# A fused attention and FFN kernel: the two loads of wk issued from ScalarE's queue instead of SyncE's

## The chip, the cores and the metric

The kernel runs on one core of a Trainium2 chip. The metric is the device time of one execution in microseconds (us), as a median over runs.

## The reference

Cut to what matters here: a cross attention with 8 heads of 128 and a context of 2 x 77 rows, then a feed-forward layer (a shared expert and a gate that is almost always shut).

```python
def _L0_xattn_ref(x, context, Wq, Wk, Wv, Wo, bo):
    q = (x @ Wq).reshape(B, Tq, h, C) * SCALE          # x is layer-normalised, 2 x 1024 x 256
    k = (context @ Wk).reshape(B, Tk, h, C) * SCALE    # context is 2 x 77 x 192
    v = (context @ Wv).reshape(B, Tk, h, C)
    attn = jax.nn.softmax(jnp.einsum('bqhc,bkhc->bhqk', q, k), axis=-1)
    out = jnp.einsum('bhqk,bkhc->bqhc', attn, v).reshape(B, Tq, h * C)
    return out @ Wo + bo
x = x + _L0_xattn_ref(_layernorm(x, axis=-1), ctx_768, ...)
x = x + _L0_ffn_ref(_layernorm(x, axis=-1), ...)
```

Wk and Wv are 192 x 1024 in float32 and Wq is 256 x 1024.

## The kernel before

Each engine runs a program of its own, written out by hand in the order in which it executes, and the engines meet at semaphores. The names: SyncE (SP) issues every load and store; TensorE (PE) multiplies; VectorE (DVE), ScalarE (ACT) and GpSimd (POOL) do the elementwise work.

The kernel has a stage of preparation (about the first 30 us of the profile) and then a loop over 16 tiles of 128 rows of x. The change lies at the very start of the preparation:

- TensorE multiplies a constant with itself 9 times (line 501), which needs no load, and then forms k for all 8 heads in `context_rows` (lines 350 and 356): for i = 0 it waits for the first load of wk, forms heads 0 to 3, waits for the second load of wk, and forms heads 4 to 7. The same is done with wv. Each of these four groups is 8 matmuls in the program. "K0", "K1", "V0" and "V1" stand for them below.
- ScalarE copies k and v out of the accumulators (lines 644 and 648). Its first instruction on the engine is the load of an activation table.
- VectorE takes the mean out of wq, in two halves (lines 929, 931 and 933), each half as soon as its load (`wqt_sb`, 512 KB) is in.
- TensorE then forms `a` = wq times k in `make_a` (line 369): heads 0 to 3 wait for the first half of wq, heads 4 to 7 for the second (`wq_ready`). ScalarE and VectorE split each `a` into two parts (lines 652 and 938), and the scores of the first tiles follow (lines 375 to 377).

The loads of this stage are issued by SyncE in the order ctx, wk (2 x 384 KB), wv (2 x 384 KB), wq (2 x 512 KB), then the first columns and rows of x, wo and the rest. Each load has a semaphore of its own, so a load that comes in earlier or later than its neighbour changes only when its own reader starts.

Of the kernel before, what the change touches and what calls it, by code (L numbers as in the profile page):

```python
# [43 lines left out]
def program(nc, x, x_t, ctx_p, wq_t, wk_p, wv_p, wo, bo, ws1, ws2, w1, w2, wr, out):  # L44
# [3 lines left out]
    HG = H // 2  # L48
    WB = wk_p.shape[2] // P
    E, _, FE = w1.shape  # L50
    DCH = D // P
    BK = B * TK
# [19 lines left out]
    with ExitStack() as ctx:  # L72
        def sb(name, shape, dt=F32):
            return ctx.enter_context(nc.sbuf_tensor(name, shape, dt))
# [4 lines left out]
        def sem(name):  # L79
            return ctx.enter_context(nc.semaphore(name))  # L80
# [34 lines left out]
        wk_sb = sb("wk_sb", [P, 2, WB, P])  # L115
# [59 lines left out]
        wk_in = [sem(f"wk_in{i}") for i in range(2)]  # L175
# [105 lines left out]
        @block.sync  # L281
        def _(sp):
            sp.dma_start(ctx_sb[:, :, :], ctx_p).then_inc(ctx_in, 16)
            for i in range(2):
                sp.dma_start(wk_sb[:, i, :, :].rearrange("p e c -> p (e c)"), wk_p[:, i, :]).then_inc(wk_in[i], 16)
            for i in range(2):
                sp.dma_start(wv_sb[:, i, :, :].rearrange("p e c -> p (e c)"), wv_p[:, i, :]).then_inc(wv_in[i], 16)
            for i in range(2):
                sp.dma_start(wqt_sb[:, i * H // 2:(i + 1) * H // 2, :],
                             wq_t.rearrange("(h p) d -> p h d", p=P)[:, i * H // 2:(i + 1) * H // 2, :]).then_inc(wq_in[i], 16)  # L290

            def load_x_t(i):
                for c in range(DCH):
                    sp.dma_start(xt_sb[:, c, :, i * GB * P:(i + 1) * GB * P],
                                 xt_rows[:, c, :, i * GB * P:(i + 1) * GB * P]).then_inc(xt_in[i], 16)

            def load_x(i):
                for b in range(B):
                    sp.dma_start(x_pairs[:, i * GB:(i + 1) * GB, b, :], x_rows[:, i * GB:(i + 1) * GB, b, :]).then_inc(x_in[i], 16)

            load_x_t(0)
            load_x(0)
            sp.dma_start(wo_sb[:, :, :], wo.rearrange("(h p) d -> p h d", p=P)).then_inc(wo_in, 16)
            sp.dma_start(wsr_sb[:, :, 0:FE], ws1.rearrange("(c p) f -> p c f", p=P)).then_inc(wsr_in, 16)
            sp.dma_start(wsr_sb[:, :, FE:NL], wr.rearrange("(c p) e -> p c e", p=P)).then_inc(wsr_in, 16)
            sp.dma_start(bo_sb[:, :], bo.rearrange("(a d) -> a d", a=1).broadcast_to([P, D])).then_inc(bo_in, 16)
            sp.dma_start(ws2_sb[:, :], ws2).then_inc(ws2_in, 16)
            for i in range(1, 4):
                load_x_t(i)
                load_x(i)  # L310

            def keep_x1(k):

                sp.wait_ge(x1_ready, 2 * k + 2)
                sp.dma_start(x1_sb[:, bass.ds(2 * k, 2), :], x1_tr[:, :, :]).then_inc(x1_kept, 16)

            def store(k):
                sp.wait_ge(y_ready, 2 * k + 2)
                sp.dma_start(out_rows[:, k, :, :], y_sb[:, bass.ds(2 * k, 2), :]).then_inc(y_out, 16)

            keep_x1(0)
            with sp.Fori(1, NB) as k:
                keep_x1(k)
                store(k - 1)
            for b in range(B):
                sp.wait_ge(y_ready, 2 * (NB - 1) + b + 1)
                sp.dma_start(out_rows[:, NB - 1, b, :], y_sb[:, 2 * (NB - 1) + b, :]).then_inc(y_out, 16)
            sp.wait_ge(y_out, 16 * (NB + 1))

            sp.wait_ge(gs, GATE_STEPS)  # L330
            any_open = sp.value_load(flag[0:1, 0:1], min_val=0, max_val=1)
            with sp.If(any_open > 0):
                sp.dma_start(w1_sb[:, :, :, :].rearrange("p e c f -> p (e c) f"),
                             w1.rearrange("e (c p) f -> p (e c) f", p=P)).then_inc(w12_in, 16)
                sp.dma_start(w2_sb[:, :, :], w2.rearrange("e p d -> p e d")).then_inc(w12_in, 16)
                with sp.Fori(0, NB) as k:
                    sp.wait_ge(r_acc, 2 * k + 2)
                    sp.dma_start(out_rows[:, k, :, :], y_sb[:, bass.ds(2 * k, 2), :]).then_inc(r_out, 16)
                sp.wait_ge(r_out, 16 * NB)
# [254 lines left out]
        def _(act):  # L594
# [43 lines left out]
            def hi_of_u(b, i):  # L638
                act.wait_ge(u_ready[b], i + 1)
                act.activation(u_hi[:, b, 2 * i:2 * i + 2, :].rearrange("p c d -> p (c d)"), u_bank[b, i][:, :], ACT.Copy).then_inc(uhi_ready[b], 1)  # L640

            for g in range(H // 2):
                act.wait_ge(kt_ready, g + 1)
                act.activation(kt_sb[:, 2 * g:2 * g + 2, :].rearrange("p h n -> p (h n)"), s_ps[:, g, 0:2 * BK],
                               ACT.Copy, scale=SCALE2).then_inc(kt_copied, 1)
# [445 lines left out]
```

## Time and profile before

| | us |
|---|---|
| median of 3 runs | 119.76 |
| lowest and highest of the runs | 119.48, 120.51 |
| the profiled execution | 119.6 |
| its span, first to last instruction | 117.8 |

The span is what the trace shows; 1.8 us of the profiled execution lie around it. In the trace TensorE is busy 110.2 us of the span, VectorE 89.2, ScalarE 85.0 and GpSimd 62.4. Starts in all rows count from the beginning of the span. A row of the trace that has a releaser ("[0.54 <-DVE wqt_sb L933]") tells how long the engine had been idle and which event ended that. A multiplication of float32 shows as two rows of TensorE.

### The profile page before, as it was taken

The page shows a single profiled execution, that of the slowest core. Times are in us where ns is not written, and L with a number is a line of the kernel's source. Part 1 is how long each engine was busy: PE and PEld are TensorE (multiplying, and loading weights), DVE is VectorE, ACT ScalarE, POOL GpSimd, SP SyncE. Part 2 cuts the span into 40 slices and gives each one's busy share as a digit, 9 for nine tenths or more (in the row PEclk, how much of TensorE's full clock was granted, in tenths as well). Part 3 has the DMA queues.
Part 4 walks back from the last instruction along what each step waited for, and adds up shares of the span by engine and source line. Part 5 has one row for each costly group of instructions (what it writes and reads, how often), then busy time and mean ns, then how long its engine had stood idle before and what let it go on. Part 6 is the DMA issues. An engine that isn't in the chain of part 4 may idle for free.

```text
span 117.8 us, 3097 instructions
## 1 busy us (share of the span) xinstructions
PE 110.2 (94%) x848; PEld 105.3 (89%) x848; DVE 89.2 (76%) x341; ACT 85.0 (72%) x346; POOL 62.4 (53%) x101
## 2 busy tenths in 40 slices
PE   6999989999899989999999999999999999989950
PEld 6988879998798889999999999999999999978940
DVE  0005999997799697887979797797979778687692
ACT  4025554699559879898998899898978989895200
POOL 2000451479607865786666577757647863429320
PEclk9999999999999999999999999999999999999998
DMA  3999999990000110022004001300400030040033
GB/s 104 341 323 362 347 327 349 351 331 34 0 6 3 49 40 0 6 103 75 0 0 178 0 0 70 108 0 0 178 0 0 37 141 3 3 178 0 26 125 116
DMA packets 11351, 12.70 MB, mean 108 GB/s; under 512 B 976, under 2 KB 9808, under 8 KB 11344
## 3 DMA queue, kind: packets, MB, share of 16 engines
q1 hardware_dynamic: 11344, 12.62, 32.4%
q8 instruction: 3, 0.05, 0.2%
q14 instruction: 4, 0.03, 0.1%
HBM read 8.42 MB, written 2.10 MB: 89 GB/s over the span
## 4 chain that ended last, share of the span: by engine, by line
PE 63%; DVE 20%; DMA 8%; issue 3%; ACT 2%; SPq 2%; DVEq 0%; ACTq 0%
PE o_ps L375 7%; PE o_ps L377 7%; PE o_ps L376 7%; PE s_ps L375 6%; PE s_ps L377 6%; PE s_ps L376 6%; DMA wqt_sb<-in_wq_t 6%; PE g_ps L431 6%; PE f_ps L461 5%; DVE ut_sb L953 3%; DVE row_max L804 2%; PE g_ps L444 2%; DVE wqt_sb L933 2%; PE f_ps L375 2%; DVE wq_mean L929 2%
## 5 line engine op out<-in xcount | busy, mean ns | idle before, releaser
L619 ACT ACTIVATE probs<-s_ps,neg_max,rstd 128x77 f32<-128x77 f32 x128 | 51.5, 425 | 8.2 <-DVE neg_max L812 8.2
L722 POOL TENSOR_TENSOR probs<-probs,recip 128x308 f32<-128x308 f32 x32 | 22.4, 701 | 24.5 <-DVE recip L818 24.3
L619 ACT ACTIVATION_READ_ACCUMULATOR probs<-s_ps,neg_max,rstd 128x1 f32 x128 | 27.3, 214 | 0.0
L375 PE MATMUL o_ps<-u_hi,pt_hi 128*128 128x256 f32 (+1 forms) x80 | 22.7, 284 | 1.1 <-DVE pt_lo L830 0.6
L377 PE MATMUL o_ps<-u_lo,pt_hi 128*128 128x256 f32 (+1 forms) x80 | 22.3, 279 | 0.0
L376 PE MATMUL o_ps<-u_hi,pt_lo 128*128 128x256 f32 (+1 forms) x80 | 22.3, 279 | 0.0
L375 PE MATMUL s_ps<-a_hi,xt_hi 128*128 128x308 f32 x64 | 22.0, 344 | 0.0
L377 PE MATMUL s_ps<-a_lo,xt_hi 128*128 128x308 f32 x64 | 19.5, 304 | 0.0
L376 PE MATMUL s_ps<-a_hi,xt_lo 128*128 128x308 f32 x64 | 19.4, 303 | 0.0
L375 PEld LDWEIGHTS o_ps<-u_hi,pt_hi 128*128 128x128 f32 (+1 forms) x80 | 15.0, 188 | 1.7 <-issue 0.8
L376 PEld LDWEIGHTS o_ps<-u_hi,pt_lo 128*128 128x128 f32 (+1 forms) x80 | 15.1, 188 | 0.0
L377 PEld LDWEIGHTS o_ps<-u_lo,pt_hi 128*128 128x128 f32 (+1 forms) x80 | 15.0, 188 | 0.0
L845 DVE TENSOR_TENSOR x_tr<-o_ps,xb_sb 128x256 f32<-128x256 f32 x16 | 6.8, 424 | 10.3 <-PE o_ps L377 10.3
L704 POOL TENSOR_TENSOR xt_lo<-xt_sb,xt_hi 128x256 fp32r<-128x256 f32 x16 | 12.5, 781 | 2.2 <-POOL xt_hi L702 0.2
L804 DVE TENSOR_REDUCE row_max<-s_ps 128x8 f32<-128x616 f32 x16 | 12.4, 775 | 0.2
L376 PEld LDWEIGHTS s_ps<-a_hi,xt_lo 128*128 128x128 f32 x64 | 12.1, 190 | 0.0
L375 PEld LDWEIGHTS s_ps<-a_hi,xt_hi 128*128 128x128 f32 x64 | 12.1, 189 | 0.0
L377 PEld LDWEIGHTS s_ps<-a_lo,xt_hi 128*128 128x128 f32 x64 | 12.0, 188 | 0.0
L726 POOL TENSOR_TENSOR xb_sb<-x_sb,bo_sb 128x256 f32<-128x256 f32 x16 | 11.7, 736 | 0.0
L431 PE MATMUL g_ps<-ident,probs 128*128 128x128 f32 x76 | 11.5, 273 | 0.2 <-POOL probs L722 0.2
L830 DVE TENSOR_TENSOR pt_lo<-g_ps,pt_hi 128x512 fp32r<-128x512 f32 x14 | 9.6, 687 | 1.6 <-ACT pt_hi L604 1.1
L604 ACT ACTIVATE pt_hi<-g_ps 128x512 fp32r<-128x512 f32 x14 | 8.4, 600 | 1.2 <-PE g_ps L431 1.2
(148 smaller groups left out, 249.1 us busy)
## 6 DMA issues: line engine op xcount, KB each, us to landing
xt_sb<-in_x_t SPq DMA_DIRECT2D x8, 256.0 KB, 6.7
x_sb<-in_x SPq DMA_DIRECT2D x8, 256.0 KB, 7.0
x_sb<-x_tr SPq DMA_DIRECT2D x8, 256.0 KB, 2.4
out<-y_sb SPq DMA_DIRECT2D x7, 256.0 KB, 2.3
wqt_sb<-in_wq_t SPq DMA_DIRECT2D x2, 512.0 KB, 7.5
wo_sb<-in_wo SPq DMA_DIRECT2D x1, 1024.0 KB, 9.4
wk_sb<-in_wk_p SPq DMA_DIRECT2D x2, 384.0 KB, 4.3
wv_sb<-in_wv_p SPq DMA_DIRECT2D x2, 384.0 KB, 5.6
```

Of the source, the lines that this page charges most:

```text
L375: pe.matmul(out_ap, hi, rhs_hi, start=first, stop=False)
L376: pe.matmul(out_ap, lo, rhs_hi, start=False, stop=False)
L377: return pe.matmul(out_ap, hi, rhs_lo, start=False, stop=last)
L431: mm = pe.transpose(to, probs[:, par, c * P:(c + 1) * P], ident[:, :])
L604: act.activation(pt_hi[:, 0:PB], g_ps[:, 0:PB], ACT.Copy).then_inc(pthi_ready, 1)
L619: e = act.activation(probs[:, par, h * TK:(h + 1) * TK], s_ps[:, 2 * par + half, (h - half * H // 2) * TK:(h - half * H // 2 + 1) * TK], A ...
L704: pool.tensor_tensor(xt_lo[:, par, :, :], src, xt_hi[:, par, :, :].bitcast(F32), ALU.subtract).then_inc(xt_ready, 1)
L722: pool.tensor_tensor(rows, rows, recip[:, par, hs].unsqueeze(2).broadcast_to([P, H // 2, TK]), ALU.mult).then_inc(probs_ready, 1)
L726: pool.tensor_tensor(xb_sb[:, par, :], x_sb[:, t, :], bo_sb[:, :], ALU.add).then_inc(xb_ready, 1)
L804: dve.tensor_reduce(row_max[:, par, :].rearrange("p (i h) -> p i h", i=2), s_ps[:, 2 * par:2 * par + 2, 0:HALF].rearrange("p i (h k) -> p ...
L830: dve.tensor_tensor(pt_lo[:, 0:PB], g_ps[:, 0:PB], pt_hi[:, 0:PB].bitcast(F32), ALU.subtract).then_inc(ptlo_ready, 1)
L845: dve.tensor_tensor(x1_tr[:, par, :], o_ps[:, 0:D], xb_sb[:, par, :], ALU.add).then_inc(x1_ready, 1)
```

## The change

The two loads of wk leave SyncE's program, where they stood between ctx and wv, and are issued by ScalarE as the first thing in its program. Their source, destination and semaphores stay the same.

```diff
         def _(sp):
             sp.dma_start(ctx_sb[:, :, :], ctx_p).then_inc(ctx_in, 16)
-            for i in range(2):
-                sp.dma_start(wk_sb[:, i, :, :].rearrange("p e c -> p (e c)"), wk_p[:, i, :]).then_inc(wk_in[i], 16)
             for i in range(2):
                 sp.dma_start(wv_sb[:, i, :, :].rearrange("p e c -> p (e c)"), wv_p[:, i, :]).then_inc(wv_in[i], 16)
...
+            for i in range(2):
+                act.dma_start(wk_sb[:, i, :, :].rearrange("p e c -> p (e c)"), wk_p[:, i, :]).then_inc(wk_in[i], 16)
             for g in range(H // 2):
                 act.wait_ge(kt_ready, g + 1)
```

At the start of ScalarE's list of instructions the difference is this (lines of the kernel's source shift by two or three between the versions; "x2" is a count):

```order
-L593 UNCONDITIONAL_BRANCH
+L591 UNCONDITIONAL_BRANCH
+L641 DMA wk_sb<-in_wk_p 128x768 x2
 L644 ACT_TABLE_LOAD
 L644 ACTIVATE kt_sb<-s_ps 128x308 x4
```

The two issues stand ahead of the load of the activation table, which was ScalarE's first instruction. SyncE's list begins like this before the change:

```order
L281 UNCONDITIONAL_BRANCH
L283 DMA ctx_sb<-in_ctx_p 128x308
L285 DMA wk_sb<-in_wk_p 128x768 x2
L287 DMA wv_sb<-in_wv_p 128x768 x2
L289 DMA wqt_sb<-in_wq_t 128x4x256 x2
L294 DMA xt_sb<-in_x_t 128x2x256 x2
```

and like this with the change:

```order
L281 UNCONDITIONAL_BRANCH
L283 DMA ctx_sb<-in_ctx_p 128x308
L285 DMA wv_sb<-in_wv_p 128x768 x2
L287 DMA wqt_sb<-in_wq_t 128x4x256 x2
L292 DMA xt_sb<-in_x_t 128x2x256 x2
```

All that stood behind wk on SyncE's queue stands two issues further ahead. The instructions of TensorE, VectorE and GpSimd are the same in both versions.

## Rows read from the trace of the kernel before

**Rows 1.** The page: busy time of each engine, and the chain that ended last.

```profile
PE 110.2 (94%) x848; PEld 105.3 (89%) x848; DVE 89.2 (76%) x341; ACT 85.0 (72%) x346; POOL 62.4 (53%) x101
...
PE 63%; DVE 20%; DMA 8%; issue 3%; ACT 2%; SPq 2%; DVEq 0%; ACTq 0%
```

**Rows 2.** The chain that ended last, 0 to 19 us: start, length, what.

```profile
3.06 6.98 DMA wqt_sb<-in_wq_t
...
10.07 1.23 DVE wq_mean L929
...
14.38 1.37 DVE wqt_sb L933
...
15.79 1.32 PE g_ps L369 x8
```

**Rows 3.** TensorE's instructions in order of time: start, length, line, operation, count.

```profile
1.06 3.88 PE L501 MATMUL f_ps<-mean_of 128*128 128x128 f32 x18 [1.06 <-DVE probs L924]
5.05 1.28 PE L350 MATMUL s_ps<-ctx_sb,wk_sb 128*128 128x154 f32 x8
...
6.99 1.31 PE L350 MATMUL s_ps<-ctx_sb,wk_sb 128*128 128x154 f32 x8
...
8.95 1.31 PE L350 MATMUL g_ps<-ctx_sb,wv_sb 128*128 128x154 f32 x8
...
10.92 0.79 PE L350 MATMUL o_ps<-ctx_sb,wv_sb 128*128 128x154 f32 x4
...
12.89 2.36 PE L369 MATMUL s_ps<-kt_sb,wqt_sb 128*128 128x154 f32 x16
15.79 1.32 PE L369 MATMUL g_ps<-kt_sb,wqt_sb 128*128 128x154 f32 x8 [0.54 <-DVE wqt_sb L933]
```

**Rows 4.** SyncE's DMA issues in order of time: start, time to issue, line.

```profile
0.74 0.39 SPq L283 DMA_DIRECT2D ctx_sb<-in_ctx_p  x1
1.19 0.89 SPq L285 DMA_DIRECT2D wk_sb<-in_wk_p  x2
2.12 0.91 SPq L287 DMA_DIRECT2D wv_sb<-in_wv_p  x2
3.06 1.51 SPq L289 DMA_DIRECT2D wqt_sb<-in_wq_t  x2
```

**Rows 5.** Loads of wk (line 285): time from issue to landing.

```profile
DMA to landing us min/median/max: 3.7/4.3/4.8
```

**Rows 6.** Loads of wv (line 287): time from issue to landing.

```profile
DMA to landing us min/median/max: 5.3/5.6/6.0
```

**Rows 7.** Loads of wq (line 289): time from issue to landing.

```profile
DMA to landing us min/median/max: 7.0/7.5/8.0
```

**Rows 8.** Stretches: engines' busy time, then granted clock, DMA engines' busy share, GB/s.

```profile
1.50:1.75 0.25, 0.25 (x3) 0.25 (x3) 0.00 (x0) 0.25 (x1) 0.07 (x1) 1.00 0.06 15
1.75:2.00 0.25, 0.25 (x3) 0.25 (x3) 0.00 (x0) 0.25 (x1) 0.00 (x0) 1.00 0.86 158
2.00:3.00 1.00, 1.00 (x7) 1.00 (x6) 0.00 (x0) 0.02 (x1) 0.00 (x0) 1.00 1.02 277
3.00:4.00 1.00, 1.00 (x7) 1.00 (x6) 0.00 (x0) 0.00 (x0) 0.00 (x0) 1.00 0.91 289
4.00:7.00 3.00, 2.90 (x23) 2.42 (x22) 0.00 (x0) 0.00 (x0) 0.00 (x0) 1.00 1.00 334
...
10.04:26.00 15.96, 15.42 (x117) 14.41 (x116) 15.21 (x34) 9.79 (x36) 6.63 (x10) 1.00 1.11 345
```

**Rows 9.** ScalarE's instructions in order of time, 0 to 15 us.

```profile
0.74 1.28 ACT L644 ACT_TABLE_LOAD   x1 [0.74 <-PEq L1085]
7.08 0.75 ACT L644 ACTIVATE kt_sb<-s_ps 128x308 f32<-128x308 f32 x2 [5.06 <-PE s_ps L356]
```

**Rows 10.** Waits of engines for loads, 10 to 30 us: total, times, longest.

```profile
POOL xt_hi L699 <- DMA xt_sb<-in_x_t: 11.5, 1, 11.5
...
ACT ws_hi L656 <- DMA ws_sb<-in_ws: 0.3, 1, 0.3
```

## The prediction

> **What bounds the kernel now.** I read the page first. TensorE is busy for 94% of the span and holds 63% of the chain that ended last; loads hold 8% of it [rows 1]. The change touches loads, so the question is where that 8% lies. The chain in order of time answers: nearly all of it is one piece, 6.98 us from 3.06 to 10.04, the first load of wq [rows 2]. Behind it comes VectorE's work on both halves of wq, without a gap from 10.07 to 15.75, and then TensorE's second half of `make_a` at 15.79. After that the chain goes through engines only. The waits for loads after 10.07 us are GpSimd's for x, which ended when its work began at 13.11 against scores that start at 17.89, and one of 0.3 us of ScalarE [rows 10]; neither is on the chain. So the change can act in the first 16 us alone, and what decides is the moment when TensorE starts the second half of `make_a`: 15.79.
>
> Two strands lead to that moment. The one on the chain is wq: landing, VectorE, 15.79. The other is TensorE itself: the warm-up of line 501 ends at 1.06 + 3.88 = 4.94, K0 starts at 5.05, K1 at 6.99, V0 at 8.95, V1 at 10.92, the first half of `make_a` at 12.89 [rows 3]. The groups follow each other every 1.96 us with no room between them. The first half of `make_a` lasts 2.36 us, to 15.25, and then TensorE waits 0.54 us for VectorE (the bracket of the last row of [rows 3]). That 0.54 us is the slack of TensorE's strand, and it is also the most that an earlier wq can give.
>
> Next, when the loads land. SyncE issues ctx at 0.74, wk at 1.19 and about 1.64, wv at 2.12 and about 2.59, wq at 3.06 [rows 4] (the second of a pair half of its 0.9 us later). With the times to landing [rows 5 to 7]: wk at 1.19 + 3.7 = 4.89 and 1.64 + 4.8 = 6.44, wv at 2.12 + 5.3 = 7.42 and 2.59 + 6.0 = 8.59, wq's first half at 3.06 + 7.0 = 10.06 (10.04 in the chain). K0 starts 0.16 us behind its load, which is also just behind the warm-up; K1 starts 0.55 us behind its load, V0 1.53 and V1 2.33.
>
> **The change part by part.**
>
> SyncE loses two issues, 0.89 us [rows 4], and wv, wq and all behind them are issued some 0.93 us sooner. wq is the load on the chain, so at first sight 0.54 us are to be had. But the loads don't wait for their issue. The DMA engines are idle until 1.75 us, 0.86 busy in the next quarter of a us, and about fully busy from 2 us until 26 [rows 8]. wq's first half is behind 154 + 4 x 384 KB of other loads, and these are the same bytes with the change, all wanted from the same engines. What can come sooner is only what the DMA engines would otherwise not have done before 1.9 us, and ctx, which starts the stream, is still issued at 0.74. I take 0 for wq's gain, with 0.54 us as its other end.
>
> The Trainium skill says the same against this change (DMA: Bandwidth & Descriptors, section "Issuing engines are not separate DMA queues"): DMAs of several issuing engines run on the same DMA engines and interleave, and only issue time of the sequencer is saved. By that rule wq gains nothing; by the count of issues alone it would gain all that TensorE's strand allows. The trace agrees so far as it goes: the DMA engines, not the issues, are full from 1.75 us on [rows 8].
>
> ScalarE gains two issues ahead of its table load. Taken at SyncE's price, 0.89 us, its table load moves from 0.74 to about 1.65 and ends at about 2.95. The copy of k that needs it starts at 7.08 [rows 9], so the cover is 4.1 us, and the cost is nothing. Without that cover it would be the 0.9 us.
>
> What moves on the path is the order in which wk and wv land. Before, wk had the DMA engines for itself, with wv behind it on the same queue. Now wk and the stream ctx, wv, wq lie on two queues and are served at the same time. No row of the trace has two queues with loads, so I bound it. The four loads of wk and wv are alike, 384 KB each, and in whatever order they are served the places at which one of them is complete stay about 4.89, 6.44, 7.42 and 8.59. The second wk can keep the second place (6.44) or fall to the last (8.59). I take the third, 7.42: ScalarE's and SyncE's first instructions start at the same 0.74 [rows 4, 9], so the first wk meets only ctx, as before, and keeps 4.89; then the second wk and the first wv share the DMA engines and both are in when the third place is reached.
>
> The sum for that: K0 starts at 5.05 as before, its weights being multiplied right behind the warm-up. K1 needs 7.42, plus the step of some 0.14 us from landing to matmul that K0 shows (4.89 to 5.05, of which the warm-up may hold a part): 7.56 in place of 6.99, 0.57 us late. V0 and V1 follow at their 1.96 us; their loads (7.42 at the latest and 8.59) are in well before 9.5 and 11.5. The first half of `make_a` ends at 15.25 + 0.57 = 15.82 in place of 15.25, and the second half starts there in place of 15.79: 0.03 us. The slack of 0.54 us takes up the rest. On the profiled execution that is 119.6 + 0.03; it stands 0.16 us under the median of the runs, which I carry along: 119.76 + 0.03, so **119.8 us**. The bounds from the same rows are -0.54 us (the second wk keeps its place and wq gains all) and, with the second wk last and the first second, the first rival's +1.2.
>
> **The rivals.**
>
> *The first wk has to share too* (slower). If ScalarE's first load gets going only when ctx is through, it shares with the first wv from its beginning, the two are complete at the second place, 6.44, and the second wk and wv at 8.59. K1 then waits until 8.59 + 0.14 = 8.73, 1.74 us late, and with 0.54 us of slack the second half of `make_a` is 1.2 us late: 121.0. If ScalarE's queue is served after all of SyncE's wv, the first wk comes at 7.42: K0 2.5 us late, less 0.54: 2.0 us, 121.7. This mechanism costs something from a second wk that lands after 7.4 or a first wk after 5.4, and over 1% from 8.6 and 6.6. For it: the DMA engines are full, and whoever shares them loses. Against it: the same start of both sequencers. The Trainium skill (the same page, section "Queues, rings and completion order") says that each DMA engine takes a packet in turn from each queue that has work. Worked out from that as an estimate, one packet of wk for one of ctx and then one for one of wv gives the third place, so 0.03 us, and the first wk is held up only if it starts late; no run here shows it yet.
>
> *wq comes sooner* (faster). If two queues fill the DMA engines better than one (from 2 to 4 us they move 277 and 289 GB/s, and 334 from 4 to 7 [rows 8], so one queue may leave something open) and wk is not pushed back, VectorE starts up to 0.54 us sooner with effect: 119.2. Against it: TensorE's strand must then not slip at all, though wk now shares.
>
> *The change doesn't do what it says.* If the table load ran first, wk would be issued at 2.02 and the first wk would land at 2.02 + 3.7 = 5.72 at best. K0 is then 0.8 us late, 0.3 us more than the slack: 120.1. The list of instructions speaks against it, the issues stand first.
>
> **How the numbers follow.** Third place, no change: 0.6, at 119.8, with 119.4 to 120.2 as its own range from the spread of the runs. The first wk shares: 0.2, at 121.0 or a little under, and wk behind all of wv 0.05, at 121.7. wq sooner: 0.1, at 119.2. Table load first: 0.05, at 120.1. A measurement of this kernel can tell about 1% (1.2 us) from no change. The faster end lies at -0.54 us, under half of that, so faster by over 1% gets 0.02, for what I have not seen. Slower by over 1% needs the second branch of the first rival, or its first with the noise against it: 0.1. Within 1%: 0.88. The range goes from the fast rival, 119.2, to the first one's price, 121.0.
>
> **What the profile of the changed kernel would show.** If I am right: K0 starts at about 5.05, the second K group about half a us late behind its load, wk's second load lands at 7.3 to 7.5 and wv's first beside it; wq's first half still lands at about 10.0 although its issue stands at about 2.1, so its time to landing grows by the 0.9 us that its issue gained; and TensorE's wait of 0.54 us ahead of the second half of `make_a` is gone, while that half starts within 0.2 us of 15.79. From there to the end all is as before. A K1 that starts after 8.5, or a K0 after 5.5, would show the first rival; a wq half that lands before 9.6 the second. The prediction would also be wrong if TensorE's clock fell in the new gap: it stays granted at 1.00 through the last gap of 0.54 us [rows 3, 8], but a gap of 1 us or more right behind the warm-up is in no row. At the lower of its two levels K1, V0 and V1 would take longer by their own 1.96 us each at most.

## The result, and the profile after

The changed kernel takes 119.36 us in the median (119.01 to 119.94, 20 runs) against 120.05 for the kernel before (119.32 to 120.51, 20 runs): a ratio of 0.9951, 95% interval 0.9934 to 0.9967. It is about 0.6 us faster, half a per cent. Within 1%, as forecast, but the forecast was no change, and the gain is clear of the measurement. The profiled execution took 119.25 us, against 119.6.

The page of the changed kernel: span, busy time, and the chain that ended last.

```profile
span 117.5 us, 3097 instructions
...
PE 109.9 (94%) x848; PEld 105.1 (89%) x848; DVE 89.3 (76%) x341; ACT 85.3 (73%) x346; POOL 62.4 (53%) x101
...
PE 70%; DVE 15%; DMA 7%; issue 2%; ACT 2%; ACTq 0%; DVEq 0%; SPq 0%
```

The load of wq has left the chain, which held 8% of loads in [rows 1]. In its place stands another load. The chain of the changed kernel, in order of time (start, length, what):

```profile
1.18 6.11 DMA wk_sb<-in_wk_p
...
7.33 1.31 PE s_ps L348 x8
...
13.30 2.29 PE s_ps L367 x16
15.60 1.05 PE g_ps L367 x8
```

The second load of wk ends at 1.18 + 6.11 = 7.29, and from there the chain goes through TensorE alone, K1, V0, V1 and both halves of `make_a`, without a piece of VectorE. TensorE's instructions in order of time (lines 350 and 369 of before are 348 and 367 here):

```profile
1.06 3.73 PE L499 MATMUL f_ps<-mean_of 128*128 128x128 f32 x18 [1.06 <-DVE probs L924]
5.22 1.29 PE L348 MATMUL s_ps<-ctx_sb,wk_sb 128*128 128x154 f32 x8 [0.43 <-DMA wk_sb<-in_wk_p]
...
7.33 1.31 PE L348 MATMUL s_ps<-ctx_sb,wk_sb 128*128 128x154 f32 x8
...
13.23 2.37 PE L367 MATMUL s_ps<-kt_sb,wqt_sb 128*128 128x154 f32 x16
15.43 1.21 PE L367 MATMUL g_ps<-kt_sb,wqt_sb 128*128 128x154 f32 x8
```

Beside [rows 3]: K0 starts 0.17 us later, since the first wk is late too (0.43 us of idle ahead of it), K1 0.34 us later, and the first half of `make_a` also 0.34 us later. The second half starts 0.36 us *sooner*, 15.43 in place of 15.79, with no wait ahead of it, and its eight rows for `g_ps` take 1.21 us in place of 1.32. So the wait of 0.54 us is gone and more than paid for. VectorE shows why it was not in the way:

```profile
9.57 1.22 DVE L929 TENSOR_REDUCE wq_mean<-wqt_sb 128x4 f32<-128x1024 f32 x1 [8.51 <-DMA wqt_sb<-in_wq_t]
...
13.87 1.36 DVE L933 TENSOR_TENSOR wqt_sb<-wqt_sb,wq_mean 128x1024 f32<-128x1024 f32 x1
```

It starts on wq at 9.57 and is through at 13.87 + 1.36 = 15.23, where [rows 2] have 10.07 and 15.75. The landings of wq and ctx (KB each, median us from issue):

```profile
wqt_sb<-in_wq_t SPq DMA_DIRECT2D x2, 512.0 KB, 7.8
ctx_sb<-in_ctx_p SPq DMA_DIRECT2D x1, 154.0 KB, 4.1
```

wq takes 7.8 us from its issue in place of 7.5 [rows 7], but is issued 0.94 us sooner. What moved is in the stretches of the changed kernel (busy time of the engines, granted clock, DMA engines' busy share, GB/s):

```profile
2.00:3.00 1.00, 1.00 (x7) 1.00 (x6) 0.00 (x0) 0.94 (x1) 0.00 (x0) 1.00 0.56 86
3.00:4.00 1.00, 1.00 (x7) 1.00 (x6) 0.00 (x0) 0.00 (x0) 0.00 (x0) 1.00 0.91 343
4.00:7.00 3.00, 2.57 (x22) 2.25 (x21) 0.00 (x0) 0.00 (x0) 0.00 (x0) 1.00 1.03 413
```

From 4 to 7 us the loads run at 413 GB/s where [rows 8] have 334, at almost the same busy share of the DMA engines, 1.03 and 1.00. The 334 is a mean over a dip: the kernel before reaches 418 GB/s too, and then falls to 277 for a microsecond, at a busy share of 1.04 and 1.08. Two stretches of before, and the second of them with the change:

```profile
5.00:5.50 0.50, 0.45 (x3) 0.48 (x4) 0.00 (x0) 0.00 (x0) 0.00 (x0) 1.00 1.04 418
5.50:6.50 1.00, 1.00 (x10) 0.84 (x10) 0.00 (x0) 0.00 (x0) 0.00 (x0) 1.00 1.08 277
```

```profile
5.50:6.50 1.00, 1.00 (x10) 0.84 (x8) 0.00 (x0) 0.00 (x0) 0.00 (x0) 1.00 1.03 412
```

So the busy share doesn't tell the rate. The changed kernel has a hole of its own: from 2 to 3 us it moves 86 GB/s, where before it was 277, and ctx lands 4.1 us after its issue in place of 2.1. Over 2 to 7 us together, hole and dip included, before and the change differ much less, 314 against 334 GB/s, which is 0.1 MB:

```profile
2.00:7.00 5.00, 4.90 (x33) 4.42 (x31) 0.00 (x0) 0.02 (x1) 0.00 (x0) 1.00 0.99 314
```

```profile
2.00:7.00 5.00, 4.57 (x32) 4.25 (x30) 0.00 (x0) 0.94 (x1) 0.00 (x0) 1.00 0.92 334
```

ScalarE's list starts as it was costed, two issues in 0.89 us and then the table load:

```profile
0.74 0.89 ACTq L641 DMA_DIRECT2D wk_sb<-in_wk_p  x2
1.66 1.28 ACT L644 ACT_TABLE_LOAD   x1 [1.66 <-PEq L1085]
```

### The profile page after: what moved, and what is told of

It reads as the page before. It is cut to its first block, busy times and chain, and to the rows that moved or that the text cites. A ratio compares the mean times of both kernels' runs of the same rounds, so it can differ in the third digit from the quotient of the medians.

```text
span 117.5 us, 3097 instructions
## 1 busy us (share of the span) xinstructions
PE 109.9 (94%) x848; PEld 105.1 (89%) x848; DVE 89.3 (76%) x341; ACT 85.3 (73%) x346; POOL 62.4 (53%) x101
## 4 chain that ended last, share of the span: by engine, by line
PE 70%; DVE 15%; DMA 7%; issue 2%; ACT 2%; ACTq 0%; DVEq 0%; SPq 0%
PE o_ps L373 7%; PE o_ps L375 7%; PE o_ps L374 7%; PE s_ps L373 6%; PE s_ps L375 6%; PE s_ps L374 6%; PE g_ps L429 6%; DMA wk_sb<-in_wk_p 5%; PE f_ps L459 5%; DVE ut_sb L953 3%; DVE row_max L804 2%; PE g_ps L442 2%; PE f_ps L373 2%; PE s_ps L367 2%; DMA x_sb<-x_tr 2%
```

## The experiments

The theories: A, two queues at once move the loads faster; B, what counts is that SyncE reaches its issue of wq 0.93 us sooner; C, the order in which wk and wv land. And on what the earlier wq meets: V, wq's landing decides through VectorE; T, TensorE's own strand, late in many executions, hides it.

Each ran beside the kernel before. The table gives, from each trace, the rate of the loads from 4 to 7 us, when VectorE starts on wq's first half and when it is through with the second, when TensorE starts the first and the second half of `make_a`, the time of that execution, and the ratio of the runs to those of before with its interval.

| kernel | GB/s | wq, VectorE | `make_a` halves | us | ratio |
|---|---|---|---|---|---|
| before | 334 | 10.07, 15.75 | 12.89, 15.79 | 119.6 | |
| the change | 413 | 9.57, 15.23 | 13.23, 15.43 | 119.25 | 0.9951 (0.9934 to 0.9967) |
| e1 one queue, alternating | 316 | 10.04, 15.65 | 13.84, 16.04 | 119.99 | 1.0002 (0.9979 to 1.0024) |
| e2 wq issued late | 323 | 10.16, 15.83 | 13.18, 15.88 | 119.91 | 1.0008 (0.9982 to 1.0033) |
| e3 issue times restored | 391 | 9.76, 15.43 | 13.57, 15.78 | 119.59 | 0.9995 (0.9973 to 1.0017) |
| e4 wv on ScalarE | 400 | 9.18, 14.85 | 16.10, 18.30 | 122.13 | 1.0158 (1.0114 to 1.0202) |
| e5 wq ahead of wv | 300 | 7.79, 14.04 | 12.87, 15.07 | 119.0 | 0.9962 (0.9942 to 0.9983) |
| e6 change, wq between wv | 402 | 8.34, 13.61 | 13.81, 16.01 | 119.82 | 0.9940 (0.9916 to 0.9964) |
| e7 one wk on ScalarE | 410 | 9.61, 15.29 | 14.09, 16.30 | 120.2 | 0.9941 (0.9917 to 0.9966) |
| e8 the change again | 412 | 9.21, 14.88 | 12.92, 15.12 | 119.11 | 0.9938 (0.9913 to 0.9962) |
| e9 table load first | 395 | 9.58, 15.28 | 13.68, 15.88 | 119.7 | 0.9962 (0.9934 to 0.9990) |
| e10 small loads on ScalarE | 326 | 9.84, 15.51 | 13.44, 15.64 | 119.63 | 0.9972 (0.9941 to 1.0003) |
| e11 ctx on ScalarE | 409 | 9.16, 14.83 | 13.74, 15.94 | 119.81 | 0.9955 (0.9926 to 0.9984) |
| e12 first wk ahead of ctx | 269 | 10.24, 15.92 | 13.27, 15.97 | 120.73 | 0.9997 (0.9976 to 1.0018) |
| e13 before again | 343 | 10.14, 15.81 | 13.64, 15.86 | 119.65 | 1.0010 (0.9984 to 1.0037) |

The rates are means over three microseconds. In all seven traces in which SyncE's queue carries ctx and all the large loads (before, e1, e2, e5, e10, e12, e13), the rate falls to between 160 and 258 GB/s in some half microsecond between 4 and 7 us. In the other eight the lowest half microsecond has 326 to 399. Over 2 to 7 us the two groups move 280 to 319 and 328 to 353 GB/s.

One rule fits all fifteen traces: the second half of `make_a` starts at the later of two times, 2.20 us after the first half (TensorE's strand) and some 0.05 us after VectorE is through. In before, e2, e12 and e13 VectorE is the later one (e13 by 0.02), in the other eleven TensorE.

**e1: one queue, the order of landing as with the change.**

```diff
-            for i in range(2):
-                sp.dma_start(wk_sb[:, i, ...], wk_p[:, i, :])...
             for i in range(2):
+                sp.dma_start(wk_sb[:, i, ...], wk_p[:, i, :])...
                 sp.dma_start(wv_sb[:, i, ...], wv_p[:, i, :])...
```

> All loads on SyncE's queue, in the order ctx, wk, wv, wk, wv, wq. Theory A (two queues at once move the loads faster: 413 GB/s from 4 to 7 us with the change against 334 before): one queue stays at about 334 GB/s, wq's first half lands at 10.0, TensorE's second half of make_a starts at about 15.8, ratio 1.00. Theory C (only the order in which wk and wv land matters): as with the change, wq at about 9.5, ratio 0.995. Theory B (wq is issued 0.93 us sooner): its issue stays at 3.06, so ratio 1.00 too.

The ratio is 1.0002 and wq comes at 10.04, so the order alone gives nothing (theory C falls). The stretch from 4 to 7 us, and TensorE's rows (e1's line 349 is 350 of before):

```profile
4.00:7.00 3.00, 3.00 (x14) 2.95 (x13) 0.00 (x0) 0.00 (x0) 0.00 (x0) 1.00 1.02 316
```

```profile
5.07 2.21 PE L349 MATMUL s_ps<-ctx_sb,wk_sb 128*128 128x154 f32 x8
...
13.84 2.36 PE L368 MATMUL s_ps<-kt_sb,wqt_sb 128*128 128x154 f32 x16
16.04 1.21 PE L368 MATMUL g_ps<-kt_sb,wqt_sb 128*128 128x154 f32 x8
```

The rate is near that of the kernel before. TensorE shows something else: K0's first eight rows took 2.21 us in place of 1.28, and its strand was so late (13.84) that it decided, though wk was in as before.

**e2: wq issued 0.9 us later, on one queue.**

```diff
             for i in range(2):
                 sp.dma_start(wv_sb[:, i, ...], wv_p[:, i, :])...
+            for i in range(2):
+                sp.dma_start(small_sb[:, i, :], ctx_p[:, 0, 0:8]).then_inc(small_in, 16)
```

> The kernel before with two loads of 4 KB between wv and wq on SyncE's queue, so that wq is issued some 0.9 us later (at about 4.0) behind the same bytes. If the loads don't wait for their issue (a step of the prediction, and theory A): wq still lands at 10.0 to 10.2, ratio 1.00 to 1.002. If the time of issue counts (theory B): wq lands at about 10.5 to 10.9, the second half of make_a starts that much later, ratio 1.004 to 1.008.

SyncE's issue of wq, and VectorE's first row on it:

```profile
4.01 1.08 SPq L293 DMA_DIRECT2D wqt_sb<-in_wq_t  x2
```

```profile
10.16 1.22 DVE L933 TENSOR_REDUCE wq_mean<-wqt_sb 128x4 f32<-128x1024 f32 x1 [9.09 <-DMA wqt_sb<-in_wq_t]
```

The issue moved from 3.06 to 4.01 and VectorE's start from 10.07 to 10.16. On one queue the loads don't wait for their issue; theory B falls there.

**e3: the changed kernel with the issue times of before.** The two small loads of e2 stand on SyncE's queue where wk stood:

```diff
             sp.dma_start(ctx_sb[:, :, :], ctx_p).then_inc(ctx_in, 16)
+            for i in range(2):
+                sp.dma_start(small_sb[:, i, :], ctx_p[:, 0, 0:8]).then_inc(small_in, 16)
             for i in range(2):
                 sp.dma_start(wv_sb[:, i, ...], wv_p[:, i, :])...
```

> The changed kernel with two loads of 4 KB on SyncE's queue where wk stood, so that wv and wq are issued at 2.1 and 3.06 as before, while wk stays on ScalarE's queue. Theory A: the stream still runs at about 400 GB/s from 4 to 7 us and wq lands at 9.5 to 9.7, ratio 0.995 to 0.997. Theory B: the gain goes with the issue times, wq lands at about 10.0, ratio 1.00.

```profile
4.00:7.00 3.00, 3.00 (x16) 2.84 (x15) 0.00 (x0) 0.00 (x0) 0.00 (x0) 1.00 1.04 391
```

The rate is that of two queues, and VectorE starts at 9.76, 0.3 us sooner than before. The two traces of the change have 9.57 and 9.21, so an earlier issue may give some 0.2 to 0.55 us once two queues run; one trace doesn't settle how much. The ratio, 0.9995, is what theory B had said, not theory A. Its interval reaches down to 0.9973, which leaves room for a gain of 0.3 us, but it doesn't meet that of the change (0.9934 to 0.9967). So the high rate without the earlier issue did not give the change's gain in time, and with two queues theory B is not ruled out. The two small loads, which also stand in SyncE's queue, may have a part in it; that was not separated. In its trace TensorE's strand decided, with 1.95 us for K0's first eight rows.

**e4: wv on ScalarE's queue, wk left on SyncE's.**

```diff
-            for i in range(2):
-                sp.dma_start(wv_sb[:, i, ...], wv_p[:, i, :])...
...
+            for i in range(2):
+                act.dma_start(wv_sb[:, i, ...], wv_p[:, i, :])...
             for g in range(H // 2):
                 act.wait_ge(kt_ready, g + 1)
```

> The kernel before with the two loads of wv, not of wk, on ScalarE's queue, first in its program. Again two queues and wq issued 0.9 us sooner. Theories A and B: wq lands at about 9.5, ratio 0.995. If it needs wk itself on the other queue (theory C, wk held back behind wv): wq lands at 10.0, ratio 1.00.

wq came at 9.18 as theories A and B said, yet the kernel lost 1.6%, which neither had expected. TensorE's rows, and stretches of the same trace (TensorE's busy time, the others', granted clock, DMA share, GB/s):

```profile
6.67 1.75 PE L348 MATMUL s_ps<-ctx_sb,wk_sb 128*128 128x154 f32 x8 [1.98 <-DMA wk_sb<-in_wk_p]
...
9.68 1.83 PE L348 MATMUL s_ps<-ctx_sb,wk_sb 128*128 128x154 f32 x8
...
16.10 2.37 PE L367 MATMUL s_ps<-kt_sb,wqt_sb 128*128 128x154 f32 x16
```

```profile
5.00:6.50 1.50, 0.00 (x0) 0.00 (x0) 0.00 (x0) 0.00 (x0) 0.00 (x0) 1.00 1.04 416
...
7.50:8.00 0.50, 0.50 (x4) 0.50 (x3) 0.00 (x0) 0.00 (x0) 0.00 (x0) 0.50 1.09 389
...
9.68:11.51 1.83, 1.83 (x12) 1.67 (x10) 1.76 (x3) 0.75 (x2) 0.00 (x0) 0.70 1.10 349
```

wk stood behind ctx on SyncE's queue, and wv had ScalarE's to itself from the start: TensorE got the first wk 1.6 us later, TensorE stood idle for 1.98 us right behind the warm-up, and the granted clock then fell from 1.00 to 0.50, the lower of its two levels (1.2 GHz). The first half of `make_a` starts at 16.10, 3.2 us late. This is the first rival of the prediction, with the clock's fall on top, brought about by the mirror image of the change.

**e5: one queue, wq's first half ahead of wv.**

```diff
+            for i in range(0, 1):
+                sp.dma_start(wqt_sb[:, i * H // 2:(i + 1) * H // 2, :],
+                             wq_t.rearrange("(h p) d -> p h d", p=P)[:, i * H // 2:(i + 1) * H // 2, :]).then_inc(wq_in[i], 16)
             for i in range(2):
                 sp.dma_start(wv_sb[:, i, ...], wv_p[:, i, :])...
-            for i in range(2):
+            for i in range(1, 2):
                 sp.dma_start(wqt_sb[:, i * H // 2:(i + 1) * H // 2, :],
```

> One queue as before, but the first half of wq is issued ahead of both loads of wv: it should land at about 7.9 in place of 10.0, wv at about 8.8 and 10.0, the second half of wq at 11.5. Theory V (the landing of wq, through VectorE, decides when the second half of make_a starts): VectorE is done by about 14.3 in place of 15.75, the second half starts on TensorE's strand at 15.1 to 15.2, ratio 0.994 to 0.995. Theory T (in most executions TensorE's own strand is late, because its clock rises only during K0, and hides what VectorE gains): ratio 0.998 to 1.00.

```profile
7.79 1.22 DVE L932 TENSOR_REDUCE wq_mean<-wqt_sb 128x4 f32<-128x1024 f32 x1 [6.73 <-DMA wqt_sb<-in_wq_t]
...
12.81 1.23 DVE L936 TENSOR_TENSOR wqt_sb<-wqt_sb,wq_mean 128x1024 f32<-128x1024 f32 x1
```

```profile
12.87 2.36 PE L372 MATMUL s_ps<-kt_sb,wqt_sb 128*128 128x154 f32 x16
15.07 1.21 PE L372 MATMUL g_ps<-kt_sb,wqt_sb 128*128 128x154 f32 x8
```

A gain of 0.4% without a second queue: wq at 7.79, VectorE through at 14.04, and the second half of `make_a` right behind the first at 15.07. So it is wq's landing, through VectorE, that the kernel before waits for (theory V). The rate stayed at 300 GB/s; the gain here is by order alone. It is smaller than theory V had said (0.994 to 0.995) and larger than theory T had (0.998 to 1.00); both act, as the last part of the next section shows.

**e6: the changed kernel with wq's first half between the two loads of wv.** On SyncE's queue of the changed kernel:

```diff
-            for i in range(2):
+            for i in range(0, 1):
                 sp.dma_start(wv_sb[:, i, ...], wv_p[:, i, :])...
+            for i in range(0, 1):
+                sp.dma_start(wqt_sb[:, i * H // 2:(i + 1) * H // 2, :], ...
+            for i in range(1, 2):
+                sp.dma_start(wv_sb[:, i, ...], wv_p[:, i, :])...
-            for i in range(2):
+            for i in range(1, 2):
                 sp.dma_start(wqt_sb[:, i * H // 2:(i + 1) * H // 2, :], ...
```

> The changed kernel with the first half of wq issued between the two loads of wv: VectorE's strand gets another 0.5 to 1 us. In the changed kernel's trace TensorE's strand decides (the second half follows the first without a wait, 15.43), bound by the landing of the second wk at 7.29. Theories A and T: nothing further, ratio 0.994 to 0.997, as the change itself. Theory V: further gain, ratio below 0.992.

VectorE in its trace:

```profile
12.38 1.23 DVE L938 TENSOR_TENSOR wqt_sb<-wqt_sb,wq_mean 128x1024 f32<-128x1024 f32 x1
15.10 2.05 DVE L943 TENSOR_TENSOR a_lo<-s_ps,a_hi 128x308 fp32r<-128x308 f32 x4 [1.49 <-ACT a_hi L657]
```

VectorE is through at 13.61, 1.6 us sooner than with the change, and then waits for ScalarE, which waits for TensorE. The ratio, 0.9940, can't be told from that of the change (0.9951, 0.9938). Beyond the change a faster VectorE strand gives nothing that these runs can tell; TensorE's bounds it.

**e7: only the first wk on ScalarE's queue.** The second is issued by SyncE behind ctx:

```diff
+            for i in range(1, 2):
+                sp.dma_start(wk_sb[:, i, ...], wk_p[:, i, :])...
...
-            for i in range(2):
+            for i in range(0, 1):
                 act.dma_start(wk_sb[:, i, ...], wk_p[:, i, :])...
```

> Only the first load of wk is issued by ScalarE; the second stays on SyncE's queue behind ctx, ahead of wv. It should land at 6.3 to 6.8 in place of 7.29, so K1 no longer waits. Theory A (two queues at once raise the rate; here only while the first wk runs): the rate from 4 to 7 us lies between 334 and 413 GB/s, wq lands at 9.7 to 10.0, ratio 0.996 to 1.00. If an early second queue is enough: wq at 9.5, TensorE's strand at 15.1 to 15.3, ratio 0.993 to 0.995.

Half of the change gives the same ratio, 0.9941, and the full rate, 410 GB/s.

**e8: the change once more.**

> The changed kernel once more, beside the others on the same chip, for a second trace of it: which of the two strands decides, and whether TensorE's clock rises at the same place. Theory T: the start of the second half of make_a moves with the clock's rise, 15.4 where it rises in the warm-up and up to 16.0 where it rises in K0. Theory V: about 15.3 to 15.5 in either case. Ratio 0.993 to 0.997 again.

TensorE and VectorE in the second trace of the changed kernel:

```profile
4.85 1.28 PE L348 MATMUL s_ps<-ctx_sb,wk_sb 128*128 128x154 f32 x8
...
7.01 1.31 PE L348 MATMUL s_ps<-ctx_sb,wk_sb 128*128 128x154 f32 x8 [0.16 <-DMA wk_sb<-in_wk_p]
...
12.92 2.36 PE L367 MATMUL s_ps<-kt_sb,wqt_sb 128*128 128x154 f32 x16
15.12 1.21 PE L367 MATMUL g_ps<-kt_sb,wqt_sb 128*128 128x154 f32 x8
```

```profile
9.21 1.22 DVE L929 TENSOR_REDUCE wq_mean<-wqt_sb 128x4 f32<-128x1024 f32 x1 [8.14 <-DMA wqt_sb<-in_wq_t]
...
13.52 1.36 DVE L933 TENSOR_TENSOR wqt_sb<-wqt_sb,wq_mean 128x1024 f32<-128x1024 f32 x1
```

VectorE started on wq at 9.21 here, 0.86 us sooner than before, and the second wk came just as TensorE came to it (a wait of 0.16 us). TensorE's strand lost almost nothing, 12.92 against 12.89, and the second half started at 15.12. The two traces of this one kernel differ by 0.3 to 0.4 us in when loads land.

**e9: the table load first.** ScalarE runs a small activation ahead of the two issues; its result is not used:

```diff
+            act.wait_ge(fill_ready, 1)
+            act.activation(small_sb[:, 0, :], mean_of[:, 0:8], ACT.Copy).then_inc(small_in, 1)
             for i in range(2):
                 act.dma_start(wk_sb[:, i, ...], wk_p[:, i, :])...
```

> The changed kernel with a small activation at the head of ScalarE's program, so that the activation table is loaded (0.74 to 2.0) before the two loads of wk are issued (at about 2.1 and 2.5). If the table load is what holds the loads back at 2 to 3 us in the changed kernel (74 to 86 GB/s there, 222 to 277 with one queue): no such hole. If two queues starting together are what does it: SyncE's loads run alone until about 3 us, then as two queues. Two queues as the cause of the higher rate: about 400 GB/s from 4 to 7 us either way. The first wk lands at 5.3 to 6.5, so K0 is 0.3 to 1.5 us late and TensorE's strand decides: ratio 0.997 to 1.006.

```profile
0.74 1.28 ACT L643 ACT_TABLE_LOAD   x1 [0.74 <-PEq L1089]
1.05 0.90 ACTq L645 DMA_DIRECT2D wk_sb<-in_wk_p  x2
```

```profile
2.00:3.00 1.00, 1.00 (x7) 1.00 (x6) 0.00 (x0) 0.23 (x2) 0.00 (x0) 1.00 0.99 233
```

ScalarE's sequencer issued wk from 1.05 on, while the table was still being loaded, and not behind it. So the rival in which the table load runs first was priced too high: K0 is 0.16 us late there, not 0.8. The hole from 2 to 3 us is gone, and the high rate follows from 4 us on (395 GB/s). Both the start of the second queue (1.05 in place of 0.74) and the table load (0.74 in place of 1.66) moved here, so e9 alone doesn't say which of them makes the hole. In e10 below the table load runs from 1.66 to 2.94, as in the change, and there is no hole (222 GB/s): the table load alone doesn't make it.

**e10, e11, e12: what the rate hangs on.** e10 leaves all loads on SyncE's queue and adds two loads of 4 KB on ScalarE's. e11 moves ctx (154 KB) to ScalarE's queue in place of wk. e12 has one queue and issues the first wk ahead of ctx. On the kernel before, the lines of e10 and e11:

```diff
+            for i in range(2):
+                act.dma_start(small_sb[:, i, :], ctx_p[:, 0, 0:8]).then_inc(small_in, 16)
```

```diff
-            sp.dma_start(ctx_sb[:, :, :], ctx_p).then_inc(ctx_in, 16)
+            act.dma_start(ctx_sb[:, :, :], ctx_p).then_inc(ctx_in, 16)
```

and of e12:

```diff
+            for i in range(0, 1):
+                sp.dma_start(wk_sb[:, i, ...], wk_p[:, i, :])...
             sp.dma_start(ctx_sb[:, :, :], ctx_p).then_inc(ctx_in, 16)
-            for i in range(2):
+            for i in range(1, 2):
                 sp.dma_start(wk_sb[:, i, ...], wk_p[:, i, :])...
```

> The kernel before, all its loads on SyncE's queue, with two loads of 4 KB issued by ScalarE at the start (and awaited at the end). If two queues must carry the large loads for the higher rate (theory A): about 330 GB/s from 4 to 7 us, wq lands at 10.0, ratio 1.00. If a second queue that is only there at the start changes how the DMA engines run (e7's rate stayed at 410 GB/s though its second queue carried only 384 KB): 400 GB/s and wq at 9.3 to 9.7, ratio 0.994 to 0.997.

> ctx (154 KB) is issued by ScalarE instead of wk; all large loads stay on SyncE's queue, 0.45 us sooner. Theory A: about 330 GB/s from 4 to 7 us; the first wk lands at 4.3 to 4.9, wq at 9.6 to 10.0, ratio 0.996 to 1.00. If a short second queue suffices: 400 GB/s, wq at 9.2 to 9.5 and wk not pushed back, TensorE's strand at about 15.1, ratio 0.993 to 0.995.

> All loads on SyncE's queue as before, but the first wk is issued ahead of ctx. The kernels whose ctx and a large load start together from two queues ran at 391 to 413 GB/s from 4 to 7 us, even where the second queue then was empty (e7, e11); those that start with ctx alone on one queue at 300 to 334. If only the head start of ctx, with its 1232-byte rows, costs the rate: about 400 GB/s, wq at 9.3 to 9.6, ratio 0.994 to 0.997. If it takes two queues that start together: about 330 GB/s, wq at 9.9 to 10.1, ratio 1.00.

The stretch from 4 to 7 us of e10 and of e11:

```profile
4.00:7.00 3.00, 3.00 (x16) 2.84 (x17) 0.00 (x0) 0.00 (x0) 0.00 (x0) 1.00 0.95 326
```

```profile
4.00:7.00 3.00, 3.00 (x14) 2.94 (x13) 0.00 (x0) 0.00 (x0) 0.00 (x0) 1.00 1.03 409
```

With small loads the rate is that of one queue; VectorE started on wq 0.23 us sooner than before all the same, and the ratio's interval (0.9941 to 1.0003) leaves a gain of up to 0.6% open. With ctx alone on the other queue it is 409 GB/s, although every large load is on SyncE's queue and ctx is in by 5 us. e12's 269 rules out ctx's head start. So theory A as I had put it, that large loads must share two queues, falls too: for the rate, a second queue with a load of 154 KB at the start is enough.

**e13: the kernel before once more.**

> The kernel before once more, for a second trace of it. Theory V with a bound by T: where TensorE's clock rises in the warm-up, VectorE decides and the second half of make_a starts at 15.7 to 16.0; where it rises late in K0, TensorE's strand decides, at 16.0 to 16.4. wq lands at 10.0 to 10.2 and the rate from 4 to 7 us is about 330 GB/s in either case. Ratio 1.00.

```profile
5.06 2.02 PE L350 MATMUL s_ps<-ctx_sb,wk_sb 128*128 128x154 f32 x8
...
15.86 1.32 PE L369 MATMUL g_ps<-kt_sb,wqt_sb 128*128 128x154 f32 x8
```

wq at 10.14 and 343 GB/s, much as in the first trace (10.07 and 334). K0's first eight rows took 2.02 us, and the two strands came together at 15.84 and 15.86.

## Why the prediction was wrong

**What bounds the kernel: right.** The start of the second half of `make_a` decides: in the changed kernel it moved by 0.36 us, the rows behind it by 0.46 (the first scores from 17.89 to 17.43), and the execution by 0.35 us.

**The step that failed: "I take 0 for wq's gain, with 0.54 us as its other end."** wq came 0.50 us sooner in one trace of the changed kernel and 0.86 in the other. The reason I gave, that the DMA engines were full from 2 us on, doesn't hold: I took the busy share of [rows 8] for the rate. In that same trace 418 GB/s went with a share of 1.04 and 277 GB/s with 1.08, and the change fills that dip (412 GB/s at 1.03). The other half of the reason, that loads don't wait for their issue, is borne out on one queue (e2: issued 0.95 us later, read 0.1 us later); on two queues e3 speaks against it.

The Trainium skill's rule that I drew on (DMA: Bandwidth & Descriptors, section "Issuing engines are not separate DMA queues") is that several issuing engines only save issue time. The runs speak against the "only": from 4 to 7 us the loads moved at 391 to 413 GB/s in the seven kernels that put ctx or a large load on the second queue, against 269 to 343 in the six that don't.

**The bound was mis-sized too.** I took TensorE's slack as the 0.54 us of its wait. Matmuls overlap: without a wait the second half starts 2.20 us after the first, not 2.36, so the slack was 15.79 - 15.09 = 0.70 us, and the rows behind a wait take 0.1 us more (1.32 against 1.21). An earlier wq was worth up to 0.8 us, of which e8 shows 0.77 (first scores at 17.12). With this slack the 0.57 us that the sum put on K1 would have cost nothing (13.46 + 2.20 = 15.66, under 15.79), not the 0.03 us of the sum.

**The landing of wk: near, and by the reason given only in part.** I put the second wk at 7.42 and K1 at 7.56; it was 7.29 and 7.33, and in e8 K1 started at 7.01 with a wait of 0.16 us for it. The second wk did come third, behind one load of wv. But the places did not stay: the first load came at about 5.1 (0.74 + 4.4) in place of 4.89, and the last, the second wv, at about 8.0 (1.64 + 6.4) in place of 8.59 (the shorter time to landing taken for the first load of each pair). K0 was 0.17 us late in one trace and 0.2 us early in the other. ScalarE's two issues cost nothing, as said.

**The rivals.** The one that came true was one that I gave 0.1, wq sooner at 119.2, with the condition that TensorE's strand must not slip at all. That condition was too strict: the strand may slip by 0.70 less what wq gains. The sharing of the first wk, which I gave 0.2, did not happen here; e4, with wv in wk's place on ScalarE's queue, shows it and the fall of the clock that I had named.

**What stays open.** Why one queue has the dips between 4 and 7 us, and two queues the hole from 2 to 3, was not settled. A load of 154 KB on the second queue at the start was enough to be rid of the dips, two of 4 KB were not, and no size between was tried. The effect lasts after that queue is empty (e7, e11). Order, ctx's head start and the table load are ruled out as its cause (e1, e12, e9). Nor is it settled how much of wq's gain is the rate's and how much the earlier issue's: the 0.1 MB more by 7 us is 0.3 us at the 357 to 364 GB/s that follow from 7 to 10 us, an estimate from these two traces, of 0.50 us gained.

K0's first eight rows took 1.25 to 1.29 us in four traces (before, the change, e5, e8), 1.75 in e4, and 1.55 to 2.27 in the other ten, of both kinds, while the granted clock reads 1.00 there in all but e4. I take it that TensorE's clock was low in a part of these rows, since rows of the same shape take 1.83 us in e4 at a granted clock of 0.70 in the mean (K1 at 9.68), but the granted clock doesn't show it. It moves TensorE's strand by up to some 1.2 us from execution to execution (13.84 in e1, 14.09 in e7, against 12.87 in e5), in the traces of e6, e7, e9 and e11 past all that wq gained.

The runs themselves show what this costs. The mean granted clock of an execution, which is on record for every run, reads 0.992 in the five traces whose eight rows took 2.02 to 2.27 us (e1, e6, e7, e11, e13) and in no other trace; it can serve as a mark of them, not as a cause, because the clock reads 1.00 in these five up to 114 us. Of the 32 runs of the changed kernel, the seven marked 0.992 or 0.993 (0.993 is in no trace) took 119.75 to 120.01 us, and the other 25 have a median of 119.11. The runs of the kernel before beside the experiments have a median of 119.9 in both groups (18 and 96 runs). This bears out theory T for about one execution in five, in which the change gains nothing, and theory V for most of the others; their medians differ by 0.8 us from the kernel before.

## What to carry to other kernels

Where a stage waits for a stream of loads, cut the stream into half microseconds and read its rate, not the busy share, before you call the DMA engines full: 277 GB/s went with a share of 1.08. If the rate has such dips, put a first load of some size on a second issuing engine, and judge by the whole stretch, because the second queue had a hole of its own here. Look at which load comes first in need: with two queues, the load that TensorE wants first belongs on the queue where nothing stands ahead of it (the change and e4 differ only in which pair of loads went there, 0.995 against 1.016). And count the slack of an engine from start to start without a wait, not from the end of one group to the start of the next.

## What the runs showed of the hardware that was not expected

- Two queues that started ctx and a large load together at 0.74 us moved 74 to 151 GB/s from 2 to 3 us, the other kernels 216 to 283, and then 391 to 413 from 4 to 7 us against 269 to 343. e9, whose second queue starts 0.3 us later, has no hole (233) and 395.
- One queue with ctx and all the large loads reached 350 to 418 GB/s in its best half microsecond between 4 and 7 us and fell to 160 to 258 in its worst, in all seven traces; with a second queue it was 418 to 435 and 326 to 399, in eight.
- ScalarE issues loads while its activation table is being loaded: from 1.05 us in e9, with the table load from 0.74 to 2.02.
- The granted clock fell to 0.50 soon after a gap of 1.98 us right behind the warm-up (e4), while 0.43 us (the change) and 0.54 us (before) left it at 1.00.
